# Products of a selective scan in buffers of their own, and the scan's inputs as three one-pass products of rounded halves

## The reference

```python
def step(state, xs):
    d_t, B_t, C_t, u_t = xs
    dA = jnp.exp(d_t[..., None] * A)
    state = dA * state + (d_t * u_t)[..., None] * B_t[:, None, :]
    y_t = jnp.einsum('bdn,bn->bd', state, C_t)
    return (state, y_t)
...
y = jnp.swapaxes(ys, 0, 1) + u * D_param
y = y * jax.nn.silu(gate)
return y @ W_out.T
```

## Time and profile before

| | |
|---|---|
| Median of 3 runs | 373.48 us (373.43 to 373.91) |
| Profiled execution | 374.15 us, of which the span of the trace 372.4 us |
| PE busy | 336.3 us (90% of the span) |
| DVE busy | 267.0 us (72%) |
| ACT busy | 206.0 us (55%) |
| POOL busy | 107.7 us (29%) |
| Scan, first to last | 84.4 to 184.0 us |
| Output projection | 182.0 to 213.1 us |
| Granted clock, mean | 0.989 of full speed |

### The profile page before, as it was taken

How to read it: one execution, slowest core, us unless ns; L and a number is a source line. 1 busy time by engine, 2 the same in 40 slices (tenths; PEclk the granted TensorE clock), 3 DMA queues, 4 the chain that set the end, 5 groups by cost and what they waited for, 6 DMA issues and landing times.

```text
span 372.4 us, 5061 instructions
## 1 busy us (share of the span) xinstructions
PE 336.3 (90%) x1928; PEld 215.4 (58%) x1928; DVE 267.0 (72%) x362; ACT 206.0 (55%) x402; POOL 107.7 (29%) x75
## 2 busy tenths in 40 slices
PE   0688999999899999999499999899999999899996
PEld 0334664653555555555165776687343577787795
DVE  2877887647979989886556698995721798975381
ACT  1985633189999999880702774463022468350350
POOL 2501000026988988888000020202000020300000
PEclk9999999999999999999699999999999999999999
DMA  6999999753030020661147799589999995000001
GB/s 243 423 422 419 420 325 422 283 212 113 2 110 6 0 113 3 225 243 46 57 127 271 285 396 400 215 329 352 393 429 363 427 422 236 2 2 2 0 2 56
DMA packets 12966, 81.85 MB, mean 220 GB/s; under 512 B 2109, under 2 KB 2365, under 8 KB 3661
## 3 DMA queue, kind: packets, MB, share of 16 engines
q1 hardware_dynamic: 11614, 78.23, 53.9%
q10 hardware_dynamic: 1296, 3.22, 2.3%
q0 software_dynamic: 32, 0.07, 0.1%
HBM read 80.86 MB, written 0.52 MB: 219 GB/s over the span
## 4 chain that ended last, share of the span: by engine, by line
PE 66%; DVE 17%; ACT 7%; DMA 6%; issue 2%; POOL 1%; SPq 0%; DVEq 0%; ACTq 0%
PE psum L1063 11%; PE psum L1002 8%; PE psum L1295 7%; PE psum L1138 7%; PE psum L1180 6%; DMA ring<-in_ctx 6%; PE psum L1215 4%; PE psum L1009 4%; PE psum L959 3%; DVE rounded L1727 3%; ACT arena L793 3%; PE psum L1414 2%; PE psum L1449 2%; PE psum L1190 2%; DVE arena L1671 2%
## 5 line engine op out<-in xcount | busy, mean ns | idle before, releaser
L793 ACT ACTIVATE arena<-arena 128x126 f32<-128x126 f32 x256 | 76.6, 394 | 3.2 <-DVE arena L1671 2.9
L1671 DVE TENSOR_TENSOR_SCAN arena<-arena,psum 128x1024 f32<-128x1024 f32 x24 | 54.6, 2281 | 5.8 <-PE psum L1138 5.0
L630 POOL TENSOR_TENSOR arena<-arena 128x1024 f32<-128x1024 f32 x23 | 54.3, 2365 | 8.4 <-DVE arena L1671 8.4
L571 POOL TENSOR_TENSOR small<-small 128x1 f32<-128x1 f32 x6 | 9.6, 1608 | 144.2 <-DVE small L1498 138.6
L1063 PE MATMUL psum<-ring,hT 128*128 128x512 f32 x104 | 50.2, 605 | 0.8 <-ACT hT L694 0.8
L1727 DVE TENSOR_TENSOR rounded<-ring,rounded 128x2048 fp32r<-128x2048 f32 x16 | 36.5, 2286 | 15.9 <-ACT rounded L820 15.9
L820 ACT ACTIVATE rounded<-ring 128x2048 fp32r<-128x2048 f32 x16 | 30.5, 1913 | 17.8 <-PE psum L1009 10.5
L1138 PE MATMUL psum<-plain 64*128 64x512 f32 x128 | 36.1, 641 | 0.4 <-DVE plain L1671 0.3
L1063 PEld LDWEIGHTS psum<-ring,hT 128*128 128x128 f32 x104 | 17.8, 190 | 21.9 <-issue 20.8
L1180 PEld LDWEIGHTS psum<-ident,arena 128*128 128x128 f32 x192 | 22.0, 141 | 11.7 <-issue 9.7
L1002 PE MATMUL psum<-rounded,split 128*128 128x512 f32 x96 | 24.7, 399 | 2.4 <-DVE rounded L1727 1.8
(11 more groups left out here) (237 smaller groups left out, 595.3 us busy)
## 6 DMA issues: line engine op xcount, KB each, us to landing
ring<-in_w_in SPq DMA_DIRECT2D x16, 1024.0 KB, 15.2
ring<-in_ctx SPq DMA_DIRECT2D x13, 1024.0 KB, 10.8
ring<-in_w_out SPq DMA_DIRECT2D x8, 1024.0 KB, 4.8
ring<-in_ctx_t SPq DMA_DIRECT2D x7, 1024.0 KB, 5.9
ring<-in_w_base SPq DMA_DIRECT2D x4, 1024.0 KB, 4.9
ring<-in_x_wk SPq DMA_DIRECT2D x4, 1024.0 KB, 9.8
ring<-in_a_wo SPq DMA_DIRECT2D x4, 1024.0 KB, 11.5
ring<-in_x_wq SPq DMA_DIRECT2D x3, 1024.0 KB, 9.0
```

Source lines behind the costliest of these rows:

```text
L630: pool.tensor_tensor(state[s % STATES], state[s % STATES], c, ALU.mult).then_inc(product_ready, 1)
L793: last = act.activation(to, of, ACT.Exp, scale=a_par[:, k, state_no:state_no + 1])
L1671: dve.tensor_tensor_scan(state[s % STATES], dA[:, s % 3, :], psum[:, p:p + 2, :].rearrange("p a b -> p (a b)"), 0.0, ALU.mult, ALU.add).th ...
```

## The change

- The scan writes one of three `state` buffers, and the product with C goes to one of three `product` buffers. The scan waits for the product three steps back instead of for the sum four steps back; the product waits for the sum three steps back.
- The product is written in another order of its axes: (n, b, t) in place of (b, n, t). A block of 128 then holds one state of both batches, so `state_sum` adds over all eight states into 128 columns, `copy_y` copies 256 columns, and `fold_y` is two plain transposes.
- `du` and `bdiag` become pairs of a rounded high tile and the rounded rest. `scan_input` is six products of rounded tiles (high x high, high x low, low x high, for each batch) in place of two float32 ones. DVE makes the rests: `du_rest`, four times, and two small operations and a second diagonal for B.
- On ACT, tanh 3 goes ahead of decay 31, `gated_high(2)` behind `high(0)`, and the load of `bk` behind the wait for product 30. On DVE `gated_low(2)` goes behind `low(0)`.

```diff
@@ -43,7 +43,7 @@
...
 DIRECT = 1
-STATES = 4
+STATES = 3
 QUAD = 4
@@ -192,7 +192,8 @@
...
         dA = carve(arena, 10336, 3, HN * P)
-        state = [plain[:, 3 * HN * P:4 * HN * P]] + [carve(arena, 13408 + HN * P * i, HN * P) for i in range(STATES - 1)]
+        state = [carve(arena, 19040, HN * P), carve(arena, 23296, HN * P), plain[:, 7 * HN * P:8 * HN * P]]
+        product = [carve(arena, 13408 + HN * P * i, HN * P) for i in range(STATES)]
         cdiag = carve(arena, 23296, NS, L)
@@ -204,8 +205,9 @@
...
         half_ones = carve(arena, 23168, P)
-        bdiag = plain[:, 0:NS * L].rearrange("p (n t) -> p n t", n=NS)
-        du = plain[:, NS * L:NS * L + DI]
+        bdiag = carve(rounded, 0, 2, NS, L)
+        du = [carve(rounded, 2 * UN * n, 2, UN) for n in (4, 5, 3, 2)]
+        b_split = carve(rounded, 6 * HN * P, 2, NS)
         sg_high = carve(arena_r, 4192 - UN, DT, P)
@@ -627,7 +630,11 @@
...
                 c = cwide[:, HN * P * (s % 2):HN * P * (s % 2) + HN * P]
-                pool.tensor_tensor(state[s % STATES], state[s % STATES], c, ALU.mult).then_inc(product_ready, 1)
+                if s >= STATES:
+                    pool.wait_ge(reduced, s - STATES + 1)
+                pool.tensor_tensor(product[s % STATES].rearrange("p (n b t) -> p b n t", n=HN, b=B),
+                                   state[s % STATES].rearrange("p (b n t) -> p b n t", b=B, n=HN),
+                                   c.rearrange("p (b n t) -> p b n t", b=B, n=HN), ALU.mult).then_inc(product_ready, 1)
                 if s % QUAD == 2 and s >= 10:
@@ -746,7 +753,7 @@
...
                 act.wait_ge(duT_psum, g + 1)
-                act.activation(du[:, UN * g:UN * g + UN], psum[:, 5, :], ACT.Copy).then_inc(du_copied, 1)
+                act.activation(du[g][:, 0, :], psum[:, 5, :], ACT.Copy).then_inc(du_copied, 1)
@@ -820,6 +827,8 @@
...
             for s in range(3, STEPS):
+                if s - 1 == GATE_AT[-1]:
+                    gate_tanh(NG - 1)
                 decay(s)
@@ -828,12 +837,10 @@
...
                     proj_copy(6)
-                if s - 1 in GATE_AT:
+                if s - 1 in GATE_AT[:-1]:
                     gate_tanh(GATE_AT.index(s - 1))
...
                     proj_copy(7)
-                if s == 30:
-                    gated_high(GATE_HALF)
                 if s == 26:
@@ -841,15 +848,18 @@
...
                     act.dma_start(bq, dram["bq"].to_broadcast([P, D])).then_inc(bias_in, 16)
-                    act.dma_start(bk, dram["bk"].to_broadcast([P, D])).then_inc(bias_in, 16)
...
+            act.wait_ge(dbu_ready, 4 * GD)
+            act.wait_ge(product_ready, STEPS - 2)
             high(0)
+            gated_high(GATE_HALF)
             act.wait_ge(gated, NB)
...
             act.wait_ge(dbu_ready, STEPS)
-            act.wait_ge(reduced, STEPS - STATES + 1)
+            act.wait_ge(product_ready, STEPS - 1)
+            act.dma_start(bk, dram["bk"].to_broadcast([P, D])).then_inc(bias_in, 16)
             high(1)
@@ -1031,7 +1041,7 @@
...
-                    pe.wait_ge(du_copied, min(j - NG + 2, NG))
+                    pe.wait_ge(du_low, min(j - NG + 2, NG))
                 if j == NB - 1:
@@ -1086,7 +1096,7 @@
...
                 if g >= 2:
-                    pe.wait_ge(du_copied, g - 1)
+                    pe.wait_ge(du_low, g - 1)
                 for k in range(GD * g, GD * g + GD):
@@ -1121,9 +1131,9 @@
...
                 if s % (2 * GD) == 0:
-                    pe.wait_ge(du_copied, s // (2 * GD) + 1)
+                    pe.wait_ge(du_low, s // (2 * GD) + 1)
                 if s == 0:
-                    pe.wait_ge(bdiag_ready, 1)
+                    pe.wait_ge(bdiag_ready, 2)
                     pe.wait_ge(c_rest, 2)
@@ -1132,11 +1142,12 @@
...
                 k = s // 2
-                left = slice(P * k, P * k + P)
+                left = slice(P * (k % GD), P * (k % GD) + P)
                 right = slice(HN * (s % 2), HN * (s % 2) + HN)
-                for b in range(B):
-                    last = pe.matmul(psum[:, input_bank(s, b), :], du[rows_of(b), left], bdiag[rows_of(b), right, :], start=True,
-                                     stop=True)
+                for n, (a, w) in enumerate(((0, 0), (0, 1), (1, 0))):
+                    for b in range(B):
+                        last = pe.matmul(psum[:, input_bank(s, b), :], du[k // GD][rows_of(b), a, left],
+                                         bdiag[rows_of(b), w, right, :], start=(n == 0), stop=(n == 2))
                 last.then_inc(dbu_ready, 1)
@@ -1173,21 +1184,19 @@
...
                     pe.wait_ge(y_skipped, q - 1)
-                for b in range(B):
-                    to = 2 * P * (s // 2 % 2) + P * b
-                    for n in range(HN // 2):
-                        of = P * HN // 2 * b + P * n
-                        last = pe.matmul(psum[:, y_bank(q), to:to + P], state[s % STATES][:, of:of + P], ident[:, :],
-                                         start=(s % 2 == 0 and b == 0 and n == 0), stop=(s % 2 == 1 and n == HN // 2 - 1),
-                                         is_transpose=True, skip_group_check=True)
+                to = P * (s // 2 % 2)
+                for n in range(HN):
+                    last = pe.matmul(psum[:, y_bank(q), to:to + P], product[s % STATES][:, P * n:P * n + P], ident[:, :],
+                                     start=(s % 2 == 0 and n == 0), stop=(s % 2 == 1 and n == HN - 1), is_transpose=True,
+                                     skip_group_check=True)
                 last.then_inc(reduced, 1)
...
                 pe.wait_ge(y_copied, q + 1)
-                for n in range(2 * B):
+                for n in range(2):
                     of = UN * (q % 2) + P * n
-                    last = pe.matmul(psum[:, y_bank(q), L * n:L * n + L], h[:, of:of + P], ident2, start=True, stop=True)
+                    last = pe.transpose(psum[:, y_bank(q), P * n:P * n + P], h[:, of:of + P], ident[:, :])
                 last.then_inc(y_folded, 1)
@@ -1641,7 +1650,11 @@
...
             dve.wait_ge(const_ready, 6)
-            dve.tensor_tensor(bdiag, wide(ident2, NS), along(ssm[:, R:R + NS], L), ALU.mult).then_inc(bdiag_ready, 1)
+            step(dve.tensor_copy(b_split[:, 0, :], ssm[:, R:R + NS]))
+            step(dve.tensor_tensor(b_split[:, 1, :], ssm[:, R:R + NS], b_split[:, 0, :].bitcast(F32), ALU.subtract))
+            for w in range(2):
+                dve.tensor_tensor(bdiag[:, w, :, :], wide(ident2, NS), along(b_split[:, w, :].bitcast(F32), L),
+                                  ALU.mult).then_inc(bdiag_ready, 1)
@@ -1657,8 +1670,14 @@
...
+            def du_rest(g):
+                dve.wait_ge(du_copied, g + 1)
+                dve.tensor_tensor(du[g][:, 1, :], psum[:, 5, :], du[g][:, 0, :].bitcast(F32), ALU.subtract).then_inc(du_low, 1)
...
             c_rest_copy(1)
+            du_rest(0)
             c_rest_copy(2)
@@ -1666,7 +1685,7 @@
...
                 if s >= STATES:
-                    dve.wait_ge(reduced, s - STATES + 1)
+                    dve.wait_ge(product_ready, s - STATES + 1)
                 p = input_bank(s, 0)
@@ -1674,14 +1693,17 @@
...
                 c = cwide[:, HN * P * (s % 2):HN * P * (s % 2) + HN * P]
-                dve.tensor_tensor(state[s % STATES], state[s % STATES], c, ALU.mult).then_inc(dve_prod, 1)
+                dve.wait_ge(reduced, s - STATES + 1)
+                dve.tensor_tensor(product[s % STATES].rearrange("p (n b t) -> p b n t", n=HN, b=B),
+                                  state[s % STATES].rearrange("p (b n t) -> p b n t", b=B, n=HN),
+                                  c.rearrange("p (b n t) -> p b n t", b=B, n=HN), ALU.mult).then_inc(dve_prod, 1)
...
                     dve.wait_ge(y_folded, q - 1)
-                dve.tensor_copy(h[:, UN * (q % 2):UN * (q % 2) + UN], psum[:, y_bank(q), :]).then_inc(y_copied, 1)
+                dve.tensor_copy(h[:, UN * (q % 2):UN * (q % 2) + 2 * P], psum[:, y_bank(q), 0:2 * P]).then_inc(y_copied, 1)
@@ -1695,6 +1717,7 @@
...
                 dve.wait_ge(y_skipped, q + 1)
+                dve.wait_ge(yg_ready, q)
                 v = slice(2 * q, 2 * q + 2)
@@ -1709,6 +1732,8 @@
...
                     times_c(s)
+                if s - 1 in DU_AT:
+                    du_rest(DU_AT.index(s - 1) + 1)
                 if s == 1:
@@ -1739,9 +1764,9 @@
...
             gate_y(STEPS // QUAD - 2)
-            gated_low(GATE_HALF)
             copy_y(STEPS // QUAD - 1)
             low(0)
+            gated_low(GATE_HALF)
             skip_y(STEPS // QUAD - 1)
```

More of the change, by code:

```diff
@@ L331, in perceiver @@
         duT_psum = sem("duT_psum")
+        du_low = sem("du_low")
         du_copied = sem("du_copied")
```

## The result

| | before | changed | forecast |
|---|---|---|---|
| median (lowest to highest), us | 373.70 (373.43 to 374.41), 4 runs | **360.11** (359.92 to 360.39), 4 runs | 358.2 (355.5 to 364.0) |
| ratio, 95% interval | | 0.9634 [0.9617, 0.9651] | |
| profiled execution, span | 374.15, 372.4 | 359.97, 358.1 | 358.9 |

What follows compares the result with a forecast made beforehand. PE was taken to bound the scan from 112.4 to 174.5 us, then a seam chain. Seam 6.6, loop 6.0, clock 2.6, folds about 1.1, less 1.0 waits: 15.3 off 374.15, 358.9 profiled, 358.2 median; range 355.5 to 364.

Steps and rivals of the forecast that it cites:

- A: Rival for the scan loop: DVE is the new bound; 358.2 us, own range 356.5 to 359.8, chance 0.60.
- B: Rival for the scan loop: PE stays the bound with scan_input at 1.06 us; 361.5 us, chance 0.15.
- C: Rival on POOL: its product is somewhat slower in the new order, 2.6 us; 361.4 us in all, chance 0.11.
- F: Rival at the seam: it closes but 3 us return in the tail, a low half late on DVE; 361, chance 0.05.
- The seam: Scan's end: silu 7 starts where scan 30 ends, 6.6 us; full clock for outputs 2.6; new waits take 1.0.
- `scan_input`: On PE: six one-pass products with overlapping halves take 0.84 us instead of 1.06, saving 0.22 a step.
- rival E: scan_input on PE: halves don't overlap on one-pass products, 1.6 us each; 373.4 us, no change, chance 0.04.
- `fold_y`: On PE: four fp32 products, 0.84 us, become two transposes, 0.3; about 1.1 us from the two folds.
- DVE's list: DVE from 112.4 us: 56.5 becomes 56.2 us, now the longest list; scan 30 ends at 168.5.
- Waits: Queues between engines: DVE's wait for POOL's product comes earlier, POOL's isn't late, du_low is done before PE needs it.
- POOL: POOL's product in the new order: 2.37 us kept, range 1.90 to 3.08; the stride rule adds nothing.
- D: Rival on POOL: its product takes 3.08 us in the new order; 375.8 us, slower than before, chance 0.05.

Runs made afterwards that it cites:

- experiment 1: Kernel before with only the ACT reordering: tanh 3 ahead of decay 31, gated_high(2) behind high(0); 366.55 us, ratio 0.9808.
- Experiment 11: Changed kernel with the old axes order, sums, copies and folds, and time_steps(3) moved behind the sum on PE; 365.23 us, ratio 0.9761.
- experiment 3: Changed kernel with scan_input as two float32 products again, without du_rest and with one B diagonal; 361.77 us, ratio 0.9681.
- experiment 9: Changed kernel with the second B diagonal made later on DVE, behind the second copy of the C part; 360.03 us, ratio 0.9622.
- experiment 8: Changed kernel with gate tiles, tanh 3 and two ACT copies earlier, and copy_y 6 ahead of scan 31 on DVE; 359.02 us, ratio 0.9598.
- experiment 4: Changed kernel without the third pair of scan_input products (low du by high B), left out of the result; 359.20 us, ratio 0.9610.
- experiment 6: Changed kernel with gate tiles, tanh 3 and two copies of ACT earlier; 359.42 us, ratio 0.9609.
- experiment 2: Changed kernel with the old ACT order: gated_high(2) at step 30, tanh 3 behind decay 31; 367.93 us, ratio 0.9846.
- experiment 5: Changed kernel with the old axes order: sums in halves, copies of 512 columns, four fold products; 365.86 us, ratio 0.9772.
- experiment 7: Changed kernel with copy_y 6 ahead of scan 31 on DVE; 359.14 us, ratio 0.9600.
- experiment 10: Changed kernel with time_steps(3) moved behind the gate tile and sum of step 6 on PE; 360.16 us, ratio 0.9625.
- experiment 12: Changed kernel with earlier tiles, copy_y 6 first, later B diagonal, time_steps(3) behind the sum, one output ahead of state_sum 29; 358.17 us, ratio 0.9573.

## Why the prediction was right, and what of it was off

The range held the time, which lies 1.9 us above the forecast. With 8.5 us it was wide enough for A, B, C and F, so that it held says little about which of them is right. A, whose number was the forecast, missed its own range (356.5 to 359.8) by 0.3. The time lies between A (DVE the new bound) and B (PE stays it), and so does the mechanism: the first half of the loop is not PE's, the second is. But PE keeps it by the length of its list, not by a `scan_input` of 1.06 us, which was B's reason. On the profiled executions 1.07 us are to be explained (359.97 for 358.9), and the end of the split products shows them whole (198.86 for 197.8).

1. **The seam**: right. 6.6 and 2.6 of the clock, less 1.0 of new waits, were forecast, 8.2 in all; 7.8 was measured as the last step and 7.0 as the first. In experiment 1 `silu` 7 comes 6.7 us earlier and three outputs take 2.5 less, 9.2 in all; off it go PE's wait for `copy_y` 6 (0.89) and 0.5 between `silu` 7 and the outputs (1.33 for 0.83), which wait for `state_sum` 29. The sum had 1.0 for both, the runs have 1.4. Rival F is out: PE's split products begin at 187.70 without a wait.
2. **`scan_input`**: the mechanism right (the halves overlap, rival E is out), the size off: 0.89 for 0.84. With three pairs at 0.22 the start-up is 0.22 too. Twenty-two of them are 1.1 us of PE's list.
3. **`fold_y`**: 0.22 to 0.24 for 0.3, as forecast and a little better. What failed is the worth put on the new order: about 1.1 us of folds in the tail and, by A, 1.5 of shorter copies on DVE's list, with nothing for the folds in the loop. Experiment 11 shows 5.1, because with the old folds PE sets nearly all of the loop.
4. **DVE's list**: 56.2 forecast, 56.01 measured up to `silu` 7. The step that failed is the one from there to the end of the scan: "it is now the longest list", so 168.5. Its lead over PE's list was called 2 us and is 1.6 by the prediction's own numbers (56.2 and 54.6). The lists were compared over the whole stretch, but PE's idle microsecond before 140 us can't be spent after it: there PE is busy for 29.43 of 29.43 us and DVE waits 1.0. In the quads of 10.5 us (measured 10.63) the prediction named this very thing as what speaks against A, and didn't put it into the sum. It is 0.9 us.
5. **Waits**: in the loop DVE's new wait for POOL's product costs nothing, as said. `du_low` was put at nothing, and PE stands 1.79 us for it once (at 101.89, before the products of `time_steps(3)`): `du_rest(1)` stands behind a scan in DVE's queue. In experiment 3, without `du_rest`, PE has no gap there. ACT bounds that stretch (25.65 of 25.80 us busy), and no more than 0.3 us is seen of it at `silu` 4. The collision of the second B diagonal with POOL's diagonal was not foreseen. The fold in the tail came at 174.13 for 172.9: 0.9 of this is `silu` 7's, 0.2 the product on DVE at 1.41 for 1.23.
6. **POOL**: right, 2377 and 2374 ns for 2365, and 2371 with plain operands. The rule of the Trainium skill (GPSIMD Engine Reference, Performance pitfalls for Q7 kernels) on inner steps over 8 bytes adds nothing here, as its wording has it: the reads have an inner step of 4 bytes and stay in memory order, only the writes have the new order in their outer steps, and it costs nothing. Rivals C and D fall.

Of what was to show it, "DVE without gap from 112 us on" holds up to about 150 us, and "PE with gaps of tenths in each step" doesn't hold: it has three before 140 us and none behind. The clock of 1.0, POOL's price and the shut seam hold.

**What stays open**: `silu` 4 starts 0.3 us later than before (112.17 for 111.85). Float32 inputs, without the second diagonal, bring it back to 111.84, and up to 94 us the later diagonal does the same (93.69 for 94.01). Whether the diagonal is all of it at `silu` 4, and why the time doesn't follow, would take an execution of experiment 9 without a slow stretch. Which of DVE and ACT bounds the first half is open too, and so is what lets the granted clock fall.

## What to carry to other kernels

Compare the lists of the engines by stretches that are as short as the buffers between them, not over a whole loop: slack of one engine in the first half does nothing in the second, and a part of the work may be worth nothing in one and its full price in the other. When an order is mended, look at what the queue holds just behind: here a copy that stood behind a scan cost 1 us until it was put ahead of it. And small gains that end at the same next wait don't add up (0.7 and 1.0 gave 1.1); the wait has to be filled too.

## What the runs showed of the hardware

- **DVE and POOL slow one another** where both read two operands from SBUF. POOL's C diagonal takes 1.90 us alone and 2.82 when it begins (76.39) inside DVE's second diagonal of B, which ends 1.06 us later; DVE's two diagonals take 2.36 together, one alone 1.23. DVE's last product takes 1.23 alone. It takes 1.41 in the change and 1.67 in experiment 8, where it begins 0.33 and 0.59 us before the end of POOL's `gate_y`, and 2.31 in experiment 4, where it begins 0.56 before the end of POOL's product and `gate_y` comes behind it. In each of these cases the one that began later grew by the time that the other still ran, less about 0.15 us. Which of them pays when a third operation follows is not settled: in experiment 4 DVE paid for `gate_y` too, in experiment 6 `gate_y` paid (1.71 for 0.72). Beside scans, which have one operand in PSUM, POOL's product keeps its 2.37. The Trainium skill (GPSIMD Engine Reference, Specifications) names this contention for DVE instructions with two inputs from SBUF; the traces agree and give the price.
- **The granted clock falls after short gaps too, in some executions.** It stands at the 1.2 GHz level for a while behind PE's gap of 1.67 us before 95 us (0.60 over 94.5 to 97 in experiment 9, 0.51 over 95 to 98 in experiment 2), or behind that of 2.03 us near 102 (0.59 over 103 to 106 in experiment 4). In the profile of the change, with gaps of 1.65 and 1.79, it doesn't. In the change and experiments 4, 5, 7 and 9, 16 of 21 executions have a mean clock of 0.994 or 0.995; in experiments 10 to 12, with the gap near 102 filled, all 13 have 0.998 or more, and so have all 8 of experiments 6 and 8, with shorter gaps (1.3 and 1.0). What decides it is not shown.
- **One-pass products on 64 rows overlap** by halves: six in 0.89 us, four in 0.66, so 0.22 a pair and 0.22 to start. A pair costs what one such product on 128 rows does (0.23).
